# Last stage of a two-layer decoder: biases folded into weight products, residual sums kept on VectorE, normalisations finished on ScalarE, four buffers for the middle result

## The reference, cut to what matters

```
x = _layernorm(x + _L1_xattn_ref(x, ctx, ...))   # 16 heads of 32, strided: head h sees context rows h, h+16, ...
x = _layernorm(x + _L1_ffn_ref(x, ...))          # binary tree of depth 8
# attention:  softmax((x Wq + bq) (ctx Wk + bk)^T / sqrt(32)) (ctx Wv + bv) Wo + bo
# tree:       gate = sigmoid((x Wq) routers^T)             255 inner nodes
#             leaf_prob = product of gate or 1-gate along each root-to-leaf path   256 leaves
#             out = (leaf_prob leaf_values) Wout + Wout_b
# layernorm:  (y - mean) / sqrt(var + 1e-5)
```

## Time and profile before

| what | value |
|---|---|
| median of 3 runs (lowest to highest) | 3124.78 us (3124.12 to 3128.44) |
| the profiled execution, its own time | 3130.56 us |
| its span, first to last instruction | 3128.8 us |
| busy PE / PEld / DVE | 2646.7 (85%) / 1869.8 (60%) / 2292.2 (73%) |
| busy ACT / POOL | 1377.8 (44%) / 552.5 (18%) |
| mean granted TensorE clock | 0.913 |

### The profile page before, as it was taken

The page is one execution under the profiler, slowest core; times in us unless marked ns, Lnnn a source line. Parts: engine busy times, 40 slices in busy tenths (PEclk is TensorE's granted clock), DMA queues, the critical chain, the costliest instruction groups (busy, mean ns, idle before and its releaser), DMA issues. The chain is left out here.

```text
span 3128.8 us, 87593 instructions
## 1 busy us (share of the span) xinstructions
PE 2646.7 (85%) x35334; PEld 1869.8 (60%) x35356; DVE 2292.2 (73%) x4033; ACT 1377.8 (44%) x2496; POOL 552.5 (18%) x659
## 2 busy tenths in 40 slices
PE   6789888888787669999999956988599999968896
PEld 5566656666666447777777633434467767646564
DVE  3888878787888517777777848969487787715987
ACT  6566656565565102222222216544355656512221
POOL 2233223332223100000000000017100000012442
PEclk9899989898998679999999987999799999978988
DMA  3001111101110140111111125539612222152321
GB/s 87 10 17 31 56 32 31 31 31 32 57 30 24 44 162 21 48 55 54 50 39 45 47 78 210 202 118 339 188 43 76 59 63 72 41 182 61 101 81 54
DMA packets 229636, 234.62 MB, mean 75 GB/s; under 512 B 24112, under 2 KB 157872, under 8 KB 229296
## 3 DMA queue, kind: packets, MB, share of 16 engines
q1 hardware_dynamic: 229296, 229.70, 22.9%
HBM read 136.84 MB, written 92.81 MB: 73 GB/s over the span
## 5 line engine op out<-in xcount | busy, mean ns | idle before, releaser
L688 ACT ACTIVATE delta_product<-delta_line,delta_conv_w 128x256 f32<-128x256 f32 x576 | 244.0, 497 | 0.0
L1221 PE MATMUL ctxatt_banks<-ctxatt_xT,ctxatt_wq 128*128 128x256 f32 x1024 | 232.4, 380 | 2.9 <-ACT ctxatt_qT L1297 2.1
L1260 PE MATMUL ctxatt_banks<-ctxatt_wo,ctxatt_oT 128*128 128x512 f32 x512 | 228.1, 599 | 4.9 <-DVE ctxatt_norm_y L1366 4.9
L1221 PEld LDWEIGHTS ctxatt_banks<-ctxatt_xT,ctxatt_wq 128*128 128x128 f32 x1024 | 189.5, 190 | 28.5 <-ACT ctxatt_qT L1297 3.3
L916 DVE TENSOR_TENSOR delta_squares<-delta_t_sys 128x30 f32<-128x30 f32 (+14 forms) x480 | 172.0, 358 | 23.6 <-issue 11.8
L919 DVE TENSOR_TENSOR delta_t_sys<-delta_t_sys,delta_squares 128x30 f32<-128x30 f32 (+14 forms) x480 | 161.5, 337 | 16.5
L427 POOL TENSOR_TENSOR delta_product<-delta_product 128x1024 f32<-128x1024 f32 x48 | 126.0, 2625 | 222.6 <-ACT delta_product L688 222.6
L1260 PEld LDWEIGHTS ctxatt_banks<-ctxatt_wo,ctxatt_oT 128*128 128x128 f32 x512 | 95.3, 191 | 115.2 <-issue 108.7
L2141 PE MATMUL wkv_banks<-wkv_woT,wkv_oT 128*128 128x512 f32 x256 | 131.6, 674 | 36.9 <-DVE wkv_oT L2339 36.9
L1307 ACT ACTIVATE ctxatt_probsT<-ctxatt_banks 128x512 f32<-128x512 f32 x128 | 69.4, 594 | 201.6 <-PE ctxatt_banks L1242 201.6
L552 PE MATMUL delta_banks<-delta_states,delta_kqT 32*32 32x32 f32 x4096 | 95.1, 202 | 61.0 <-issue 61.0
(11 more groups left out here) (333 smaller groups left out, 6526.9 us busy)
## 6 DMA issues: line engine op xcount, KB each, us to landing
h<-ffn_hid SPq DMA_DIRECT2D x66, 256.0 KB, 2.0
ffn_hid<-h SPq DMA_DIRECT2D x6, 1536.0 KB, 9.0
wkv_xT<-xT SPq DMA_DIRECT2D x64, 129.0 KB, 2.9
delta_xT<-xT SPq DMA_DIRECT2D x64, 128.0 KB
delta_x<-x SPq DMA_DIRECT2D x16, 512.0 KB
xT<-delta_newT SPq DMA_DIRECT2D x64, 128.0 KB
x<-delta_new SPq DMA_DIRECT2D x16, 512.0 KB
ctxatt_xT<-xT SPq DMA_DIRECT2D x64, 128.0 KB, 2.6
```

The source lines that it names most:

```text
L688: made = act.activation(slot(n, i)[:, j - 1, g].rearrange("p (b t) -> p b t", b=B), line[:, i, g, :, j:j + P], ACT.Copy, scale=conv_w[:, i ...
L1221: mm = pe.matmul(b_q[:, i * B * P:(i + 1) * B * P], wq[:, k, pair * P:(pair + 1) * P], xT_sb[:, n.parity, k], start=k == 0, stop=k == KB - 1)
L1260: mm = pe.matmul(b_o[:], oT[:, b, k, :], wo[:, k, :], start=k == 0, stop=k == PAIRS - 1)
```

## The change

The two output biases no longer get added by POOL to a whole tile. `bo` enters the product `vo`, scaled by 1/16 (the 16 heads' probabilities of one token sum to 16), and `wb` enters `lo` (the leaf probabilities sum to 1), each as one more product of one row; the two broadcasts of the biases over 128 partitions become loads of one row. `x_bo` and `mid_wb` are gone, so DVE sums from `x` and from `mid`, and `mid` gets four buffers, for which the loops of PE, ACT, DVE and POOL have four steps in their body (`pipelined_by_four`: steps 0 to 7 written out, the loop passes twice). Both norms are `ScaledNorm`s: POOL's `root` has four small operations and ACT applies the norm. The scores' bias is one product for both sequences. PE's and ACT's orders within a step are new; DVE sums the attention two places earlier.

```diff
-        CTX_LOADS, ATTENTION_LOADS, TREE_LOADS = 5, 3, 6
+        CTX_LOADS, ATTENTION_LOADS, TREE_LOADS = 5, 4, 5
-        mid = sb("mid", [P, 2, B, D])
-        midb = sb("mid_wb", [P, 2, B, D])
+        mid = sb("mid", [P, 4, B, D])
-        norm_a, norm_f = Norm(m, "norm_a", B), Norm(m, "norm_f", B)
+        norm_a, norm_f = ScaledNorm(m, "norm_a", B), ScaledNorm(m, "norm_f", B)
@@ POOL's step(n) @@
                     if t := n.back(5):
-                        norm_f.root(pool, t, eps, half)
-                    if t := n.back(3):
...
-                            pool.tensor_tensor(midb[:, t.parity, b], mid[:, t.parity, b], wb_rep[:], ALU.add).then_inc(midb_done, 1)
-                    if n:
...
-                            pool.tensor_tensor(xb_sb[:, n.parity, b], x_sb[:, n.parity, b], bo_rep[:], ALU.add).then_inc(xb_done, 1)
+                        norm_f.root(pool, t, eps, half, zero)
                     if t := n.back(1):
-                        norm_a.root(pool, t, eps, half)
+                        norm_a.root(pool, t, eps, half, zero)
...
-                        jobs.append((D, [(kv[1][:, e, b, :], mats["woT"][:, e, :]) for e in range(KB)]))
+                        jobs.append((D, [(kv[1][:, e, b, :], mats["woT"][:, e, :]) for e in range(KB)] + [(share_row[:], bo_row[:])]))
...
-                        jobs.append((D, [(leafT[:, e, l * P:(l + 1) * P], mats["outT"][:, e, :]) for e in range(KB)]))
+                        jobs.append((D, [(leafT[:, e, l * P:(l + 1) * P], mats["outT"][:, e, :]) for e in range(KB)] + [(ones_row[:], wb_row[:])]))
...
                 def scores(n):
+                    pe.matmul(b_s[:, 0:B * CTX], ones_row[:], qk_bias[:].rearrange("p b n -> p (b n)"), start=True, stop=False)
                     for b in range(B):
-                        pe.matmul(to, ones_row[:], qk_bias[:, b, :], start=True, stop=False)
@@ PE's step(n) @@
+                    if n:
+                        scores(n)
                     if t1:
                         turn_probabilities(t1)
                     if t4:
                         turn_leaves(t4, t3)
-                    if n:
-                        scores(n)
-                    if t4:
-                        feed(t4)
                     if t2:
                         turn_mid(t2, 0)
                     if t1:
                         attend(t1)
                     if t2:
                         turn_mid(t2, 1)
                         gates(t2, 0)
+                    if t4:
+                        feed(t4)
+                    if t2:
                         gates(t2, 1)
@@ ACT's step(n) @@
+                    if t5:
+                        finish_tree(t5, 0)
+                        finish_tree(t5, 1)
+                    if t1:
+                        keep_turned_probabilities(t1)
+                    if t4:
+                        keep_turned_leaves(t4)
+                    if t2:
+                        keep_turned_mid(t2, 0)
+                    if n:
+                        exps(n)
+                    if t2:
+                        keep_turned_mid(t2, 1)
+                        gate_leaves(t2)
+                    if t1:
+                        finish_attention(t1, 0)
+                        finish_attention(t1, 1)
@@ DVE's step(n) @@
-                        if t5 and i in (8, 9):
-                            finish_tree(t5, b)
-                        if t1 and i in (10, 11):
+                        if t1 and i in (8, 9):
                             sum_attention(t1, b)
-                        if t1 and i in (12, 13):
+                        if t1 and i in (10, 11):
                             norm_a.statistics(dve, t1, b)
-                        if t1 and i in (14, 15):
+                        if t1 and i in (12, 13):
                             norm_a.aggregate(dve, t1, b)
                     if n:
                         soften(n)
-                    for b in range(B):
-                        if t1:
-                            finish_attention(t1, b)
```

More of the change, by code:

```diff
@@ L53, in pipelined, with pipelined_by_four @@
         step(Tile(pair * 2 + (first + 1), (first + 1) % 2, steps, first + 1))
+    for n in range(steps, steps + lag):
+        step(Tile(n, n % 2, steps, n))
+def pipelined_by_four(eng, steps, lag, step, more=1):
+    first = lag + more + (steps - lag - more) % 4
+    for n in range(first):
+        step(Tile(n, n % 2, steps, n))
+    with eng.Fori(0, (steps - first) // 4) as four:
+        for k in range(4):
+            step(Tile(four * 4 + (first + k), (first + k) % 2, steps, first + k))
     for n in range(steps, steps + lag):
@@ L2446, in strided_attention_and_tree @@
         ones_row = sb("ones_row", [1, P])
-        banks = [ps(f"bank{i}", [P, 512]) for i in range(8)]
+        share_row = sb("share_row", [1, P])
+        zero = sb("zero", [P, B])
+        all_banks = ps("banks", [P, 8, 512])
+        banks = [all_banks[:, i] for i in range(8)]
         mats = {k: sb(k, [P, KB, D]) for k in ("wkT", "wvT", "wq", "woT", "fq", "outT")}
@@ L2692, in keep_products @@
                     act.wait_ge(ready, 3)
-                def step(n):
[L2695 to L2707, removed]
-                    if n:
[L2709 to L2718, removed]
@@ new lines, in keep_turned_mid, with exps @@
+                def keep_turned_mid(n, b):
+                    if b == 0:
+                        wait(act, gated, n, B, 0)
+                    wait(act, midT_made, n, B, b + 1)
+                    act.activation(midT[:, b], b_T[:], ACT.Copy).then_inc(midT_kept, 1)
+                def exps(n):
+                    wait(act, shifted, n, SHIFT_OPS, SHIFT_OPS)
+                    wait(act, softened, n, SOFT_OPS, -SOFT_OPS)
+                    act.activation(e_sb[:, n.parity], s_sb[:, n.parity], ACT.Exp).then_inc(exped, 1)
@@ new lines, in gate_leaves, with finish_attention @@
+                def gate_leaves(n):
+                    wait(act, gated, n, B, B)
+                    wait(act, gate_done, n, 1, 0)
+                    act.activation(th[:], b_g[:], ACT.Tanh, scale=0.5).then_inc(th_done, 1)
+                    wait(act, th_done, n, 1, 1)
+                    wait(act, tree, n, TREE_OPS, 0)
+                    act.activation(gate[:].rearrange("p b n -> p (b n)"), th[:], ACT.Identity, bias=center[:], scale=0.5).then_inc(gate_done, 1)
+                def finish_attention(n, b):
+                    wait(act, midT_made, n, B, -B)
+                    wait(act, norm_f.done, n, norm_f.OPS, norm_f.SUMMED - 4 * norm_f.OPS)
+                    norm_a.finish(act, n, b, mid[:, n.quarter, b])
@@ new lines, in finish_tree @@
+                def finish_tree(n, b):
+                    gone(act, stored, n, 16)
+                    norm_f.finish(act, n, b, o_sb[:, n.parity, b])
+                def step(n):
+                    t1, t2, t4, t5 = n.back(1), n.back(2), n.back(4), n.back(5)
+                    if t5:
[7 more added lines that the diff above has]
+                        keep_turned_mid(t2, 0)
+                    if n:
+                        exps(n)
[5 more added lines that the diff above has]
+                        finish_attention(t1, 1)
@@ L2720, in _ @@
                 keep_products()
-                pipelined(act, STEPS, LAG, step)
+                pipelined_by_four(act, STEPS, LAG, step)
             @block.vector
@@ L2761, in soften @@
                     c.end()
[L2763 to L2767, removed]
-                def finish_attention(n, b):
-                    wait(dve, midT_made, n, B, -B)
-                    wait(dve, midb_done, n, B, -B)
-                    norm_a.finish(dve, n, b, mid[:, n.parity, b])
                 def walk_tree(n, i):
@@ L2788, in walk_tree, with sum_attention @@
                         dve.tensor_tensor(right, path[:, :, 0:nodes], gate[:, :, nodes - 1:2 * nodes - 1], ALU.mult).then_inc(tree, 1)
+                def sum_attention(n, b):
+                    if b == 0:
+                        here(dve, x_here, n, 16)
+                    wait(dve, norm_a.finished, n, B, b + 1 - B)
+                    wait(dve, attended, n, B, b + 1)
+                    dve.tensor_tensor(norm_a.y[:, b], b_o[:, b], x_sb[:, n.parity, b], ALU.add).then_inc(norm_a.done, 1)
                 def sum_tree(n, b):
-                    wait(dve, norm_f.done, n, norm_f.OPS, 0)
-                    wait(dve, midb_done, n, B, b + 1)
+                    wait(dve, norm_f.finished, n, B, b + 1 - B)
                     wait(dve, fed, n, B, b + 1)
-                    dve.tensor_tensor(norm_f.y[:, b], b_f[b][:], midb[:, n.parity, b], ALU.add).then_inc(norm_f.done, 1)
-                def finish_tree(n, b):
-                    gone(dve, stored, n, 16)
-                    norm_f.finish(dve, n, b, o_sb[:, n.parity, b])
+                    dve.tensor_tensor(norm_f.y[:, b], b_f[:, b], mid[:, n.quarter, b], ALU.add).then_inc(norm_f.done, 1)
                 def step(n):
```

(5 more changed lines are left out.)

70 lines of the change are left out of this document (37 added, 33 removed).

## The result

The changed kernel takes 3189.6 us (median of 4 runs, 3179.55 to 3190.1), the kernel before 3126.61 us in the same comparison: ratio 1.0183, 95% interval 1.016 to 1.0205. It is slower, by 63 us; 80 us were forecast (3205 us). The profiled execution took 3189.81 us, its span is 3188.0 us against 3128.8.

The account below looks back on a forecast made before the run. DVE, slightly ahead of PE, was taken as the bound; a new loop through ACT plus clock loss gives 22.2 us steps. Steps +77.6, weights +3.5, fill -8, end +7: about +80, median 3205 us, range 3140 to 3235.

Parts of the forecast that it names:

- What bounds the kernel before: Steady stretch: DVE and PE near their bound together, DVE slightly ahead and held up by POOL; 16.1 us a step.
- The loop through ACT's head: Steps 5 to 17: ACT's first instruction, norm f's finish, waits for POOL and DVE, blocking copies PE needs; 18.6 us a step.
- The clock: PE's 5.6 us pause before `turn_mid` starts every step at the lower clock level; 3.6 us lost a step.
- the 21 to 23 named as a sign: Step length in us that the changed profile would show, beside a granted clock of 0.75 to 0.85.
- The fill: Steps 0 to 4, before any finish of norm f, the loop still open: -8 us, between 0 and -16.
- Weight products: Four more products of 512 columns on PE, two instructions each of 0.43 us: +3.5 us.
- The end: From step 18's walk to the last finish: 29.4 us against 22.0, so +7 us (0 to +12).
- the loop without the clock: Rival: the loop sets 18.6 us a step, no clock loss; 3155 us, chance 0.17.
- The change that pays: Rival: the finish's wait never ends last, PE sets a step of 13.6 us; 3088 us, chance 0.13.

Follow-up runs that it names:

- the kernel with the clock held up: Six products without use put on PE in the pause before `turn_mid`, against the changed kernel: 3168.42 us, ratio 1.0112 to the kernel before.

## Why the prediction was right, point by point

- **What bounds the kernel before** (DVE, held up by POOL, with PE close behind): right, and shown. With POOL's additions gone and DVE's own work and order as before, finishes and path operations fall to the forecast durations; with PE's new order beside it the step falls to 13.6 us, near PE's 13.0. What the prediction left out is that the 16.1 us hold some clock already: by DVE's first walk operations, steps 7, 10, 12 and 15 of the kernel before take 17.1 to 18.9 us, each with the granted clock at 0.50 from close to its start on, and the other steps from 5 to 14 take 15.5 to 15.8.
- **The loop through ACT's head**: right in place and in size. 18.6 us were summed; the kernel with the clock held up has 18.8. PE's pause was forecast at 5.6 us and is 5.3 to 6.0 in steps 5 to 15; in steps 16 and 17, which have no scores to fill part of it, it is 8.5 and 8.0. Moving the head away opened the loop, lengthening the head lengthened it. ACT's rule of order, from the Trainium skill ("TensorE: Matmul & The Clock Gate", Architectural detail), is what the sum stood on: the trace agrees, with ACT idle for 48.6 us in 13 steps while copies whose inputs were ready stood behind.
- **The clock**: the mechanism was right, the size was not. The term of 3.6 us a step measured 1.9 (20.6 less 18.8), and this alone is 13 x 1.7 = 22 us too much; for the same reason the step of 20.6 us lies under the 21 to 23 named as a sign, while the granted clock of 0.83 lies within its 0.75 to 0.85. The lower level was granted within the pause. In step 12, windows of 1 us of PE alone, then PE's timeline:

```profile
3033.00:3034.00 1.00, 0.00 (x0) 1.00 0.00 0
3034.00:3035.00 1.00, 0.00 (x0) 0.74 0.00 0
3035.00:3036.00 1.00, 0.00 (x0) 0.50 0.00 0
...
3040.00:3041.00 1.00, 1.00 (x3) 0.50 0.00 0
3041.00:3042.00 1.00, 1.00 (x4) 0.84 0.00 0
```
```profile
3038.07 1.09 PE L2614 MATMUL tree_banks<-tree_ident,tree_mid 128*128 128x128 f32 x4 [5.99 <-ACT tree_leafpT L2708]
...
3047.44 1.89 PE L2630 MATMUL tree_banks<-tree_wr,tree_midT 128*128 128x256 f32 x8
```

  The level falls at about 3034.5, 2.4 us into the pause, and comes back at about 3041.3. Of these 6.8 us, 3.6 lay in the pause, where they cost nothing; 3.2 were paid at half speed, 1.6 us lost: 11.3 us from `turn_mid` to the gates' end, against 9.7. In step 5 the level fell only at 2891.1, 4.3 us into the pause; there these products took 12.6 us, 2.9 us lost. I had taken losses from pauses of 3.1 and 3.6 us, behind which 9.7 and 5.5 us of the lower level were still to come, and the first of them belonged to a low stretch of 10.2 us; the 1.9 us measured lie under both. What the Trainium skill ("TensorE: Matmul & The Clock Gate", "HAM oscillation") describes, a wait in every tile that begins every tile throttled, was so here: the lower level came in each of the 13 pauses.
- **The fill**: -17.2 us against -8, a little outside its bound of -16. In steps 1 to 4 PE had work at once and its clock stayed up (0.96 against 0.79), which I had not counted. The size is not firm: the changed kernel run again takes 50.4 us here (-13) at a granted clock of 0.86, so the 4 us between the two executions go along with the clock, and the other kernels with scores first, the one with added products apart, take 43 to 51 us. What of the rest is order and what is clock was not separated.
- **Weight products**: +4.8 against +3.5. A one-row product of 512 columns took 1.05 us for its two instructions, not 0.86; with four of them that is 0.8 of the 1.3 us, and the rest was not looked into.
- **The end**: +8.7 against +7.
- **The rivals**: the loop without the clock (3155 us) is what the products in the pause come near, at 3168 us. The change that pays (3088 us) is what it becomes with ACT's order mended, 3086 us; the step of 13.6 us assumed for it was 13.8.

Not tried: the norms on ACT with POOL's additions still there, PE's new order with nothing else changed, and whether the single bias product of the scores alone has a measurable effect.

## What to carry to other kernels

Before an instruction is moved to an idle engine, follow its wait back: if what it waits for is made in the same step, everything behind it in that engine's order inherits the wait, and if any of that leads back to the waited-for work, the step's length is the length of that loop, however idle the engines are. Put such an instruction behind what others need, ahead of a wait that comes later anyway. And when an engine's ordinary operations take over twice their undisturbed time, look at what runs beside them first: the version that took POOL's additions away and left the norms on DVE had all of the gain here.

## What the runs showed of the hardware

- A pause of PE costs by how much of the lower clock (0.50) is left when PE resumes. In step 12 the lower clock began 2.4 us into a pause of 6.0 us and lasted 6.8 us, 1.6 us lost; in step 5 it began 4.3 us into a pause of 5.3, 2.9 us lost. A longer pause was not cheaper: with pauses of 6.7 to 7.5 us the step grew by 1.7 us for 1.4 put in. Filling the pause with 5.2 us of useless products kept the clock at 1.00 and made the kernel 22 us faster.
- DVE's finish of a norm (128x512) took 545 ns where POOL had no whole-tile additions and 1263 ns on average where it had them. The same finish as an activation with scale and bias on ACT takes 805 ns in the changed kernel, where those additions are gone; no run shows it beside them.
